# Routing of an expert layer: whole token rows scattered into expert regions in place of a table, a sort and gathers

## The reference, cut to what matters

```python
z = x1 @ W.T + adapter(x1)                 # 512 features, an adapter of rank 16 for each sequence
logits = z @ gate_w.T                      # 8 experts
top2 = the two largest logits of a token; shares = softmax over these two
out = x1                                   # residual
for e in range(8):                         # F = 352
    h = silu(z @ gate_proj[e].T) * (z @ up_proj[e].T)
    out += share_of(e) * (h @ down_proj[e].T)   # share 0 where e is not among the two
```

## Time and profile before

| | |
|---|---|
| runs | 1233.03, 1235.46, 1237.46 us (median 1235.46) |
| profiled execution | span 1234.8 us; the page gives no other time of its own |
| `adapted_layer` | 514 to about 715 us |
| `experts` | about 720 to 1224 us |
| busy share | PE 90%, POOL 60%, DVE 49%, ACT 41% |
| mean DMA rate | 144 GB/s |

### The profile page before, as it was taken

One profiled execution on the slowest core, in us unless ns is written; L12 is line 12 of the kernel. 1 busy time (PEld: TensorE's weight loads), 2 busy tenths in 40 slices (PEclk: granted clock), 3 DMA queues, 4 the chain that ended last, 5 costly groups with the idle time before them and its releaser, 6 DMA issues. The chain is left out here.

```text
span 1234.8 us, 34930 instructions
## 1 busy us (share of the span) xinstructions
PE 1113.7 (90%) x12488; PEld 1033.8 (84%) x12489; DVE 609.1 (49%) x1161; ACT 504.3 (41%) x994; POOL 739.4 (60%) x1083
## 2 busy tenths in 40 slices
PE   2589999999999998788988839999999999999996
PEld 2578998999989998688987839989898989899995
DVE  8846777766777764434434613333333333333332
ACT  3246777776777665344334212222222222222221
POOL 6668898998998986013333424555555545454554
PEclk9869999999999999688989969999999999999999
DMA  6044455554554543733533245475656565744444
GB/s 260 25 128 154 151 207 179 179 184 159 182 202 160 195 135 118 290 133 114 182 115 103 70 143 134 89 205 126 170 123 174 117 180 112 185 73 80 76 76 68
DMA packets 65921, 177.70 MB, mean 144 GB/s; under 512 B 12656, under 2 KB 21752, under 8 KB 62304
## 3 DMA queue, kind: packets, MB, share of 16 engines
q1 hardware_dynamic: 40736, 127.65, 29.6%
q0 software_dynamic: 19200, 38.94, 17.5%
q10 hardware_dynamic: 5952, 10.65, 2.4%
HBM read 105.84 MB, written 71.38 MB: 144 GB/s over the span
## 5 line engine op out<-in xcount | busy, mean ns | idle before, releaser
L1733 POOL TENSOR_TENSOR idle<-small 128x1 f32<-128x1 f32 x284 | 94.7, 333 | 205.6 <-DMA out<-result,scatter_at 106.8
L965 POOL TENSOR_TENSOR in_lo<-inner,in_hi 128x512 fp32r<-128x512 f32 x128 | 175.8, 1374 | 46.3 <-ACT in_hi L1113 46.0
L1807 PE MATMUL banks<-slots,zt_hi 128*128 x568 | 190.6, 335 | 4.8 <-issue 1.7
L1809 PE MATMUL banks<-slots,zt_lo 128*128 x568 | 183.7, 323 | 0.0
L1808 PE MATMUL banks<-slots,zt_hi 128*128 x568 | 182.9, 322 | 0.0
L1201 DVE TENSOR_TENSOR inner<-silu,banks 128x512 f32<-128x512 f32 x128 | 87.6, 684 | 129.4 <-ACT silu L1108 125.9
L1909 DVE TENSOR_TENSOR hid<-silu_g,banks 128x352 f32<-128x352 f32 x71 | 37.0, 521 | 208.3 <-PE banks L1809 208.3
L1756 POOL DMA_INDIRECT out<-result,scatter_at x71 | 113.7, 1601 | 23.9 <-issue 18.8
L1807 PEld LDWEIGHTS banks<-slots,zt_hi 128*128 128x128 f32 x568 | 107.2, 189 | 7.4 <-issue 7.2
L1808 PEld LDWEIGHTS banks<-slots,zt_hi 128*128 128x128 f32 x568 | 107.7, 190 | 0.0
L1108 ACT ACTIVATE silu<-banks 128x512 f32<-128x512 f32 x128 | 76.3, 596 | 76.0 <-PE banks L1034 74.0
(11 more groups left out here) (249 smaller groups left out, 3392.1 us busy)
## 6 DMA issues: line engine op xcount, KB each, us to landing
late_dram<-split_part SPq DMA_DIRECT2D x32, 816.0 KB, 4.3
slots<-late_dram SPq DMA_DIRECT2D x24, 1088.0 KB
raw_part<-in_late_w SPq DMA_DIRECT2D x16, 816.0 KB
x_t<-in_x_t SPq DMA_DIRECT2D x16, 512.0 KB, 3.4
x_both<-in_x_tok SPq DMA_DIRECT2D x16, 512.0 KB, 6.0
x_both<-in_x_res SPq DMA_DIRECT2D x16, 512.0 KB, 3.3
x1t_dram<-x_both SPq DMA_DIRECT2D x16, 512.0 KB, 6.0
x<-x1t_dram SPq DMA_DIRECT2D x16, 512.0 KB
```

The source lines that it names most:

```text
L965: nc.gpsimd.tensor_tensor(in_lo[:, cs, :], inner[u % 2][:, :, :], in_hi[:, cs, :].bitcast(F32), ALU.subtract).then_inc(in_done, 1)
L1733: nc.gpsimd.tensor_tensor(idle[:, at:at + 1], small[:, 0:1], small[:, 0:1], ALU.add)
L1807: nc.tensor.matmul(psum[bank][:, 0:FD], zt_hi[:, k, :], w_high, start=(k == 0), stop=False)
L1809: ins = nc.tensor.matmul(psum[bank][:, 0:FD], zt_lo[:, k, :], w_high, start=False, stop=(k == DK - 1))
```

## The change

`z_dram`, `table_dram`, their padding, `columns`, the sort, the gathers and PE's `transpose_z` are gone.

- A region now has 34 blocks, and `rows_dram` holds for each pair the whole row: 512 values of z and then four words (token, best expert, share of the best, share of the second), 2080 bytes. DVE's `enter` writes these four words over the logits in `z_out`; POOL scatters `z_out` rows themselves, two indirect DMAs of 128 rows for each sub tile, each pair issued once ACT has copied the sub tile.
- The rows behind each expert's last token are filled with blank rows: SP writes one block of 128 per expert with a plain DMA at a row number that it loads from `ctl`.
- In `experts`, ACT fetches each block with plain DMAs at a loaded row number (`fetch_z`: 4 of 64 KB, each for 32 partitions, so that partition q*32+n holds features of chunk q of rows n, n+32, n+64 and n+96) and one for the four words (`fetch_meta`). DVE's `turn` transposes all 32x32 squares of the [128, 512] tile straight into one of two banks; the order of features that results is matched by a fixed permutation of the expert weights' rows on the host. `zt_hi` and `zt_lo` have two buffers each. `set_share` picks the share of the block's expert by three small DVE instructions.
- Orders: ACT's body is `high_h(j-1)`, `high_z(j+1)`, `gate(j)`, `fetch_z(j+2)`, `fetch_meta(j)`; DVE's is `turn(j+1)`, `low_h(j-1)`, `low_z(j+1)`, `multiply(j)`, `set_share(j-1)`, `weigh(j-1)`; PE's is `transpose_h(j-1)`, `gate_up(j)`, `down(j-1)`. The row of the padding block that idle fetches read is written in `prepare` in place of three smaller paddings.

```diff
 adapted_layer, SP, behind the loop:
+                sp.wait_ge(pads_ready, 1)
+                for e in range(NE):
+                    first_pad = sp.value_load(ctl[0:1, PAD_AT + e:PAD_AT + e + 1], min_val=e * REGION * P, max_val=e * REGION * P + TOK)
+                    sp.dma_start(rows_dram[bass.ds(first_pad, P), :], blank_rows).then_inc(pads_stored, 16)
 adapted_layer, POOL:
                     pool.wait_ge(entries_ready, t + 1)
-                    nc.gpsimd.tensor_tensor(idle[:, 0:1], small[:, 0:1], small[:, 0:1], ALU.add).then_inc(idle_done, 1)
-                    for k in range(2):
-                        for s in range(LSUB):
-                            nc.gpsimd.indirect_dma_start(table_dram, bass.IndirectOffsetOnAxis(ap=row_i[b][:, k, s:s + 1], axis=0),
-                                                         entry[b][:, s, k, :], None).then_inc(entries_stored[b], 16)
+                    for s in range(LSUB):
+                        pool.wait_ge(drained[Z[s % 2][0]], use(t, s) + 2)
+                        nc.gpsimd.tensor_tensor(idle[:, s:s + 1], small[:, 0:1], small[:, 0:1], ALU.add).then_inc(idle_done, 1)
+                        for k in range(2):
+                            nc.gpsimd.indirect_dma_start(rows_dram, bass.IndirectOffsetOnAxis(ap=row_i[b][:, k, s:s + 1], axis=0),
+                                                         z_out[b][:, s, :], None).then_inc(rows_stored[b], 16)
 adapted_layer, ACT:
-                def store(t, b):
...
-                    act.dma_start(z_tiles[bass.ds(t, 1)].rearrange("a p s h -> p (a s) h"), z_out[b][:, :, 0:D]).then_inc(z_stored[b], 16)
 experts, POOL:
-                def gather(j, b):
...
-                    nc.gpsimd.indirect_dma_start(z_now[b][:, :], None, z_dram,
-                                                 bass.IndirectOffsetOnAxis(ap=gather_at[b][:, 0:1], axis=0)).then_inc(z_loaded[b], 16)
+                def set_scatter(j, n, b):
+                    pool.wait_ge(meta_loaded[b], 16 * (n + 1))
                     alone()
+                    nc.gpsimd.tensor_copy(scatter_at[b][:, :], meta[b][:, 0:1]).then_inc(scatter_set, 1)
 experts, PE:
-                def transpose_z(j, n, b):
-                    pe.wait_ge(z_loaded[b], 16 * (n + 1))
...
-                def gate_up(j, slot):
-
-                    pe.wait_ge(drained[ZT], j + 2)
+                def gate_up(j, b, slot):
+
+                    pe.wait_ge(zt_low, j + 1)
 experts, ACT:
+                def row_of(j):
+                    return act.value_load(ctl[0:1, bass.ds(j + ROW_AT, 1)], min_val=0, max_val=BLANK * P)
+
+                def fetch_z(j, b):
+
+                    act.wait_ge(z_turned, j - 1)
+                    block_rows = rows_dram[bass.ds(row_of(j), P), 0:D].rearrange("(a n) (q h) -> q n a h", a=QUADS, q=QUADS)
+                    for q in range(QUADS):
+                        act.dma_start(z_quads[b][q * QUAD:(q + 1) * QUAD, :, :], block_rows[q]).then_inc(z_loaded[b], 16)
...
+                def high_z(j, b):
+                    act.wait_ge(z_turned, j + 1)
+                    nc.scalar.activation(quads(zt_hi[b]), turned_z(b), ACT.Copy).then_inc(zt_high, 1)
+
+                def body(j, n, b):
+                    high_h(j - 1)
+                    act.wait_ge(filled[UP], j)
+                    high_z(j + 1, 1 - b)
+                    gate(j)
+                    fetch_z(j + 2, b)
+                    fetch_meta(j, b)
 experts, DVE:
+                def turn(j, n, b):
+                    dve.wait_ge(z_loaded[b], 16 * QUADS * (n + 1))
+                    nc.vector.transpose(psum[ZT[b]][:, :], z_quads[b][:, :, :].rearrange("p a h -> p (a h)")).then_inc(z_turned, 1)
...
                 def body(j, n, b, first):
+                    turn(j + 1, n + b, 1 - b)
                     low_h(j - 1)
+                    low_z(j + 1, 1 - b)
                     multiply(j)
-                    low_z(j + 1)
+                    set_share(j - 1, n - 1 + b, 1 - b)
                     weigh(j - 1, n - 1 + b, 1 - b, first)
```

More of the change, by code:

```diff
@@ L206, in index_constants @@
     small[:, 1] = p // RANK
-    for c in range(3):
-        small[:, 2 + c] = p + c * P
     small[:, 5] = p + 1
@@ L1270, in adapted_layer @@
         gap, expo, total = sb("gap", [P, LSUB]), sb("expo", [P, LSUB]), sb("total", [P, LSUB])
-        row_i, entry = [sb(f"row_i{b}", [P, 2, LSUB], I32) for b in range(2)], [sb(f"entry{b}", [P, LSUB, 2, 2]) for b in range(2)]
-        taken, free = PLACES + 2 * COLS + NE + CHUNKS * COLS, [(DK + 3) * D]
+        row_i = [sb(f"row_i{b}", [P, 2, LSUB], I32) for b in range(2)]
+        taken, free = PLACES + CTL + COLS, [(DK + 3) * D]
         def spare(*shape):
@@ L1301, in adapted_layer @@
         gap_ready, expo_ready, entries_ready = (sem(n) for n in ("gap_ready", "expo_ready", "entries_ready"))
-        entries_stored = [sem(f"entries_stored{b}") for b in range(2)]
+        rows_stored = [sem(f"rows_stored{b}") for b in range(2)]
+        pads_ready, pads_stored = sem("pads_ready"), sem("pads_stored")
         LINKS = 21
@@ L1680, in experts @@
+def experts(nc, alloc, sem, psum, ident, small, idle, slots, weights_loaded, load_expert, rows_dram, out,
+            ctl, expert_f, ctl_ready):
     with ExitStack() as scope:
         sb = alloc(scope)
-        columns = sb("columns", [P, CHUNKS, P, 2])
-        row_of, share_of = sb("row_of", [P, COLS], I32), sb("share_of", [P, COLS])
-        z_now = [sb(f"z_now{b}", [P, D]) for b in range(2)]
-        gather_at = [sb(f"gather_at{b}", [P, 1], I32) for b in range(2)]
+        z_quads = [sb(f"z_quads{b}", [P, QUADS, P]) for b in range(2)]
+        meta = [sb(f"meta{b}", [P, META]) for b in range(2)]
+        share_parts, share = sb("share_parts", [P, 2]), sb("share", [P, 1])
@@ L1844, in body @@
                     wait_weights(j)
-                    gate_up(j, now)
-                    transpose_z(j + 1, n + b, 1 - b)
+                    gate_up(j, b, now)
                     down(j - 1, n - 1 + b, 1 - b, slot_of(j - 1))
-                transpose_z(0, 0, 0)
                 first = slot_of(0)
                 wait_weights(0)
-                gate_up(0, first)
-                transpose_z(1, 0, 1)
+                gate_up(0, 0, first)
                 with pe.Fori(0, BLOCKS // 2) as k:
@@ L1870, in gate @@
                     nc.scalar.activation(silu_g[:, :], psum[GATE][:, 0:FD], ACT.Silu).then_inc(drained[GATE], 1)
-                def high_z(j):
-                    act.wait_ge(filled[ZT], j + 1)
-                    nc.scalar.activation(zt_hi[:, :, :].rearrange("p k n -> p (k n)"), psum[ZT][:, :], ACT.Copy).then_inc(zt_high, 1)
-                high_z(0)
-                gate(0)
-                high_z(1)
-                with act.Fori(1, BLOCKS) as j:
-                    high_h(j - 1)
-                    gate(j)
-                    high_z(j + 1)
+                def high_z(j, b):
[8 more added lines that the diff above has]
+                    fetch_meta(j, b)
+                act.wait_ge(ctl_ready, 1)
+                for j in range(2):
+                    block_rows = rows_dram[bass.ds(row_of(j), P), 0:D].rearrange("(a n) (q h) -> q n a h", a=QUADS, q=QUADS)
+                    for q in range(QUADS):
+                        act.dma_start(z_quads[j][q * QUAD:(q + 1) * QUAD, :, :], block_rows[q]).then_inc(z_loaded[j], 16)
+                act.dma_start(meta[0][:, :], rows_dram[bass.ds(row_of(0), P), D:D + META]).then_inc(meta_loaded[0], 16)
+                high_z(0, 0)
+                high_z(1, 1)
+                fetch_z(2, 0)
+                gate(0)
+                high_h(0)
+                act.wait_ge(filled[UP], 1)
+                high_z(2, 0)
+                gate(1)
+                fetch_z(3, 1)
+                act.dma_start(meta[1][:, :], rows_dram[bass.ds(row_of(1), P), D:D + META]).then_inc(meta_loaded[1], 16)
+                body(2, 1, 0)
+                with act.Fori(1, BLOCKS // 2) as k:
+                    body(2 * k + 1, k, 1)
+                    body(2 * k + 2, k + 1, 0)
                 high_h(BLOCKS - 1)
@@ L1949, in laid_out @@
     flat = lambda w, n: w.reshape(NE, n, P, -1).transpose(0, 2, 1, 3).reshape(NE, P, -1)
-    experts_w = np.concatenate([flat(gate.transpose(0, 2, 1), DK), flat(up.transpose(0, 2, 1), DK), flat(rows, FC)], 2)
+    turned = np.arange(D).reshape(QUADS, DK, QUAD).transpose(1, 0, 2).reshape(-1)
+    experts_w = np.concatenate([flat(gate.transpose(0, 2, 1)[:, turned], DK), flat(up.transpose(0, 2, 1)[:, turned], DK), flat(rows, FC)], 2)
     arrays = {
```

214 lines of the change are left out of this document (97 added, 117 removed).

## The result

| | before | after |
|---|---|---|
| median of the runs | 1234.41 us (4 runs, 1233.03 to 1237.46) | 1216.12 us (4 runs, 1215.06 to 1224.15) |
| span of the profiled execution | 1234.8 us | 1213.3 us |
| ratio after to before | | 0.9876, 95% interval 0.9844 to 0.9908 |

The account below looks back on a forecast made before the run. The prediction took PE's order of work in the expert stage, 6.73 us per block, as the bound. From a span of 1234.8 us, -28.4 - 9 + 24 + 6 - 1 = -8.4 gave 1226.4, as median 1227.1 us; range 1202 to 1268.

Parts of the forecast that it names:

- TensorE's z transposes go: Expert stage, PE: each block loses 0.40 us (0.35 to 0.44), period 6.33 us; over 71 blocks -28.4 us.
- The irregular 10.1 us go: Expert stage: irregular time goes with the gathers that caused most of it, -9 us (bounds -10 and 0).
- The fetch ring: Expert stage: fetch, `turn`, `high_z`, `gate` and next fetch take 6.30 us, against PE's 6.33; PE still sets the pace.
- Weight loads: Five loads inside the expert loop make fetches late, 2.2 us each for three fetches: +24 us (bounds 0 and +57).
- Rival B: Expert stage: weight loads hardly touch the fetches, 0.8 us extra per fetch; 1203 us, chance 0.20.
- The first load: Start of the expert loop: a weight load without waits holds up two or three fetches, +6 us (bounds 0 and 12).
- Between the stages: From the adapted layer's last copy to `gate_up(0)`: later POOL issues, no table, sort or gather; -1 us (bounds -6, +5).
- The adapted layer: Stage ahead of the experts: more rows written while DMA has room, smaller paddings, dropped store; 0 (bounds -1 and +3).
- C: Expert stage: the fetch ring is the bound, 6.80 us per block in place of 6.73; 1269.5 us, chance 0.24.
- E: Expert stage: VectorE's transpose is slow, `turn` 1.38 us in place of 0.69, ring 6.99; 1282.5 us, chance 0.08.
- One sign of C: Expert stage: every period over 6.4 us, PE waiting for DVE throughout, chain through DMAs into `z_quads`, PE busy under 90%.
- D: Whole kernel: the parts cancel, with 3.3 us extra per fetch during weight loads; 1237.6 us, chance 0.06.

Follow-up runs that it names:

- a_dummy: The changed kernel with four transposes of the identity, results unused, put back on PE between `gate_up` and `down`: 1230.81 us.
- a_early_lookup: The changed kernel with PE's two value loads (slot and loaded count) moved ahead of `transpose_h`: 1207.63 us.
- a_ahead: The changed kernel with each fetch of z issued one block earlier, in the same place of ACT's order: 1196.74 us.
- b_idle: The kernel before, both table entries of a sub tile issued together, one small POOL instruction ahead of each pair, no new wait: 1222.07 us.
- b_paced: The kernel before, POOL waiting for ACT's copy of each sub tile and running a small `tensor_tensor` ahead of each pair of table entries: 1220.54 us.
- a_best: The changed kernel with early value loads, fetches a block earlier, first in-loop weight load held for two more fetches, small POOL instruction ahead of every scatter: 1172.39 us.

## Why the prediction was right, and where it was not

The forecast was faster, 1227.1 us in a range of 1202 to 1268; measured 1216.12. The direction came out right and the time inside, at the lower edge of the forecast's own 1216 to 1240, but that is luck. For the expert stage I had forecast -7.4 us, and it took 0.8 more; for the adapted layer 0, and it gave 16.7. Without that gain the two spans, taken from the first copy on, would differ by 1.5 us the other way: no change. The sum of -8.4 us was made of terms that missed in both directions, and the largest gain was in none of them.

1. *TensorE's z transposes go, -28.4.* The transposes cost a block 0.45 us (a_dummy 6.71 against a_early_lookup 6.26), a little over the 0.44 that I had as a bound. But the period fell only from 6.73 to 6.54: 70 x 0.19 = -13 us. The step that failed is the sentence "Nothing on PE takes their place: the value load that followed them is there as before". It looked at the value load behind the transposes and not at the two ahead of `gate_up`, which had run while PE still had `down` and 0.35 us of transposes to do. With the cover gone 0.31 us of them came to light in the block shown, and 0.28 of a block on average (6.54 against 6.26). It could have been read before: `hid` was ready 1.81 us ahead of `transpose_h`, and the lookups take 1.43.

2. *The irregular 10.1 us go, -9.* Over 70 periods before, 482.6 - 471.1 = 11.5 us were irregular, and with their gathers they did go.

3. *The fetch ring, 6.30 us.* It was no bound at a period of 6.54: a_ahead, which loosens it, has the same quiet periods. In a_early_lookup at 6.26 DVE waits for most fetches, the sign of a ring just about as long as the block. `turn` took 0.726 us (I had 0.69), `high_z` in squares 0.598 (0.60). The issue of the first fetch to the start of `turn` is 4.0 to 4.5 us, where 1.57 + 2.40 = 3.97 was my sum; the value load on ACT took 0.3 us and not 0.57. The terms erred against each other: with 0.47 for `gate` the measured ones add up to 6.1 to 6.6, around my 6.30.

4. *Weight loads, +24.* Measured 20.5 us, with PE's waits for `ht_lo` behind a late `turn`, once for each load, as described; they are 1.8 to 3.0 us long, not 4 to 6, and the period is lengthened by 4.1 us per load in all. One fetch of each load is 4 to 5 us late and the next two 0 to 2, not 2.2 each, which comes to nearly the same. What I left out is the clock, which falls behind a wait of 3 us. The worst fetch of each load took 8.1 to 9.4 us from issue to use, where quiet ones took 4.0 to 4.5. The Trainium skill's rule in "DMA: Bandwidth & Descriptors" ("Queues, rings and completion order"), that an engine drains a whole packet before it changes queues, fits these numbers; no row shows the packets change. Rival B, by which the loads hardly touch the fetches, is out.

5. *The first load, +6.* Measured 5.0 over the first three periods, where before the first alone had 1.4 too much.

6. *Between the stages, -1.* 17.1 us from the last copy to `gate_up(0)` both before and after. The terms were -1 with bounds -6 and +5. POOL did keep up with ACT, because its scatters go out as the copies come: the last ends 3.1 us behind the last copy. The equal numbers hide a gain: before, the last copy was itself held back behind POOL's last issue, and from that issue the way shrank from 18.5 to 14.0 us.

7. *The adapted layer, 0 (bounds -1 and +3).* Here lay the gain: -16.7 us. I had the stage down as "in which DMA has room" and asked of POOL's issues only when the last one ends. (The 33 MB of rows written there are a slip too: 8192 rows of 2080 bytes are 17 MB.) The timeline of before shows ACT, in five places, waiting 3.7 to 6.7 us for a semaphore of an engine that had long been done; one of them is in the earlier trace rows, `[6.67 <-remote]`. I read over it because its releaser had no name. b_idle shows that it hangs on what POOL does between its issues; the term put at nothing was worth about 12 us to the kernel.

8. *The other rivals and the signs.* No block was slower than before's in the quiet stretches, so neither C nor E came to pass. One sign of C did come, every period over 6.4 us, and one of being wrong, a clock of 0.98 in the stage; the first was the value loads, not the ring, since PE waits for its own stream 45 times and for `ht_lo` five times. `turn` started 0.7 us behind `gate_up`, as forecast. D, that the parts cancel, is what the expert stage did, but with bare value loads in place of fetches 3.3 us late. E's slow transpose is refuted by its own row:

```profile
L1890 DVE STREAM_TRANSPOSE banks<-z_quads 128x512 f32<-128x512 f32 x16 | 11.6, 726 | 2.0 <-DMA z_quads<-rows_dram 1.8
```

The estimate from the Trainium skill's "VectorE: DVE Perf Modes" ("The three transpose paths") was 1.24 us for the same 128x512 values; the measurement decides, 0.726. The rule of that page's "Rules for kernel authors", to transpose on TensorE where PSUM will do as destination, would, by the periods of a_dummy and a_early_lookup, have cost 0.45 us per block here.

Within the expert stage alone, items 1 to 5 as measured give -13 - 11.5 + 20.5 + 5.0 = +1.0 us, and the loop was 0.8 us longer.

## What to carry to other kernels

When work leaves the bounding engine, look for what its own instruction stream does under that work (value loads, register arithmetic) and ask how long each would stand bare; moving them ahead of the wait was worth 8 us here and nothing before the change. A fetch belongs at the earliest place that its buffer allows, not where it is first convenient: one block earlier gave 19 us. And a long idle time without a named releaser is a finding, not noise: set it beside what every other engine does at that moment. A stretch that gets 19 us shorter need not give 19 us: look for what the next stage waits for once it is gone.

## What the hardware showed that was not expected

- While POOL issues indirect DMAs back to back, semaphore updates of PE (and of ACT and DVE) can come late: a matmul that ended at 574.37 us raised its semaphore at 578.92, 1.2 us behind the end of POOL's last issue. In the first layer, where POOL does arithmetic, of 269 updates of PE between 40 and 500 us that can be told apart only one is over 0.8 us late (1.23 us). A `tensor_tensor` of 0.2 us between the pairs (b_idle) took the copies' stretch from 178.6 to 159.8 us and the kernel from 1232.3 to 1222.1. In the last two tiles holds of 3.2 to 4.9 us stayed with such instructions in place, in every kernel that has them (b_paced, b_idle, after, a_best and those between).
- In the expert stage, with one or two indirect DMAs per block, no such hold was found in the quiet stretches, though POOL issued 140 of them before.
- VectorE's 32x32 transposes of a 128x512 float32 tile from SBUF straight into a PSUM bank took 0.726 us, ACT's copy that reorders its squares 0.598 us, no more than the plain one.
- After PE had waited 3.02 us, the third to the ninth matmul stepped by 0.43 in place of 0.23 us (granted clock 0.63): seven steps of 0.20 us make 1.4 us on top of the wait.
